# Expert coefficients by SBUF-to-SBUF transfers, the y chain in PSUM, and a new order of the loop

## What is computed

```
h = layernorm(x) * (1 + ca) + sa
q, k, v = h @ Wq + bq, h @ Wk + bk, h @ Wv + bv        # 16 heads of 8 channels
o = softmax(causal(q k^T / sqrt(8))) v
y = o @ Wo + bo
x = x + ga * (layernorm(y) * gamma + beta)
h = layernorm(x) * (1 + cb) + sb
p = softmax(h @ router)                                # 8 experts, the two largest kept: coef[t, e]
x = x + gb * (sum over e of coef[t, e] * (silu(h @ gate_e) * (h @ up_e)) @ down_e + shared expert)
```

## Time and profile before

| | us |
|---|---|
| three runs | 608.85, 610.38, 613.12 |
| median | 610.38 |
| the profiled execution's own time | 609.45 |
| its span, first to last instruction | 607.4 |
| TensorE busy | 521.5 |
| VectorE busy | 409.6 |
| ScalarE busy | 286.8 |
| GpSimd busy | 242.9 |

### The profile page before, as it was taken

The page is one execution under the profiler, slowest core; times in us unless marked ns, Lnnn a source line. Parts: engine busy times, 40 slices in busy tenths (PEclk is TensorE's granted clock), DMA queues, the critical chain, the costliest instruction groups (busy, mean ns, idle before and its releaser), DMA issues.

```text
span 607.4 us, 10186 instructions
## 1 busy us (share of the span) xinstructions
PE 521.5 (86%) x3627; PEld 277.3 (46%) x3635; DVE 409.6 (67%) x904; ACT 286.8 (47%) x582; POOL 242.9 (40%) x298
## 2 busy tenths in 40 slices
PE   1657798899998998889989998899989998999566
PEld 1523344454544464444544454455545464446234
DVE  6467875686677748787578757776778656873154
ACT  1103264645365555656354545565465636355311
POOL 6034115624274345623462427524562414242410
PEclk9956697989998999999998999999999999699769
DMA  5172313411233013411332113401341131001000
GB/s 139 55 183 76 108 41 76 144 41 40 64 92 123 12 47 81 146 32 41 93 121 63 41 50 84 144 2 43 89 145 41 41 74 42 2 2 37 0 1 17
DMA packets 46930, 40.65 MB, mean 67 GB/s; under 512 B 8088, under 2 KB 42656, under 8 KB 46880
## 3 DMA queue, kind: packets, MB, share of 16 engines
...
...
## 4 chain that ended last, share of the span: by engine, by line
PE 64%; DVE 19%; ACT 6%; issue 4%; POOL 3%; DMA 2%; SPq 1%; DVEq 0%; POOLq 0%
PE pv_bank L1023 10%; PE s_bank L1009 10%; PE s_bank L994 10%; DVE row_max L815 7%; PE gate_bank L1074 6%; PE gate_bank L1105 6%; PE up_bank L1083 5%; PE misc L952 4%; PE s_bank L996 4%; ACT probs L639 3%; PE misc L974 3%; DVE y_sb L851 2%; DVE stats_x L760 2%; ACT square L665 2%; PE misc L1045 1%
## 5 line engine op out<-in xcount | busy, mean ns | idle before, releaser
L815 DVE TENSOR_REDUCE row_max<-s_bank 128x1 f32<-128x512 f32 (+3 forms) x352 | 212.6, 636 | 47.0 <-PE s_bank L996 45.3
L639 ACT ACTIVATE probs<-s_bank 128x512 f32<-128x512 f32 x320 | 177.6, 595 | 54.4 <-PE s_bank L1009 51.6
L994 PE MATMUL s_bank<-k_stack,q_stack 72*128 72x256 bf16 (+3 forms) x512 | 139.1, 320 | 25.1 <-DVE row_max L815 13.9
L547 POOL TENSOR_SCALAR_AFFINE_SELECT probs<-probs 128x512 f32<-128x512 f32 (+1 forms) x96 | 77.6, 811 | 154.3 <-ACT probs L639 154.1
L1009 PE MATMUL s_bank<-q_stack,k_stack 75*128 75x128 bf16 (+3 forms) x512 | 115.0, 310 | 14.5 <-ACT probs L639 12.1
L996 PE MATMUL s_bank<-causal,ident_bf 128*128 128x128 bf16 x512 | 103.8, 229 | 0.0
L994 PEld LDWEIGHTS s_bank<-k_stack,q_stack 72*128 72x128 bf16 x512 | 51.9, 101 | 99.7 <-DVE row_max L815 66.3
L1023 PE MATMUL pv_bank<-probs,v_aug 128*32 128x512 f32 (+3 forms) x1024 | 95.3, 471 | 1.0
L1009 PEld LDWEIGHTS s_bank<-q_stack,k_stack 75*128 75x128 bf16 x512 | 40.0, 100 | 55.3 <-ACT probs L639 40.6
L648 ACT ACTIVATE u_sb<-pv_bank 128x512 f32<-128x512 f32 x32 | 19.1, 596 | 92.1 <-PE pv_bank L1023 92.1
L996 PEld LDWEIGHTS s_bank<-causal,ident_bf 128*128 128x128 bf16 x512 | 52.6, 103 | 15.7 <-issue 9.2
...
## 6 DMA issues: line engine op xcount, KB each, us to landing
...
```

Source lines behind the costliest of these rows:

```text
L547: nc.gpsimd.affine_select(out=view, in_=view, compare_op=ALU.is_ge, fill=0.0, base=0, pattern=pat, channel_multiplier=-1).then_inc(probs_r ...
L639: nc.scalar.activation(dst, src, ACT.Exp, scale=SCALE).then_inc(exp_done, 1)
L815: nc.vector.reduce_max(row_max[s % 2][:, 0, h:h + nh, qt], s1_bank[u % 2][:, 0:nh * w].rearrange("p (h k) -> p h k", h=nh), AX_X).then_inc ...
L994: nc.tensor.matmul(dst[:, w * i:w * (i + 1)], q_stack[0:KROWS, h, P * qt:P * (qt + 1)], k_stack[0:KROWS, h, 0:w], start=True, stop=False)
```

## The change

1. Coefficients. GpSimd's split is gone. PE transposes coef itself in float32 into rows 0 to 7 of misc, ACT copies these to coef_T (8 rows of 512). A new task cb on SyncE issues four transfers, one for each expert block: each reads two rows of coef_T, each row 64 times, and writes 128 rows of coef_b, 256 KB. The products with pick, ACT's copies to coef_sb and pick itself are gone. GpSimd (in the last batch DVE) multiplies hidden by coef_b when the block's own transfer has landed.
2. The y chain. PE first writes the bias into up_bank with one product of 65 rows of bfloat16 parts, then adds o @ Wo to it. ACT squares from the bank and also scales from the bank by the inverse deviation; DVE multiplies by gamma in one instruction (yg). u0 waits until y has left the bank.
3. The router product has 8 columns in place of 128.
4. The order: 30 steps in a slot in place of 15, s1, s2 and pv placed slot by slot, other tables EXTRA, LAST and LATER.

```diff
-    3: {0: [("c0", "prev")], 2: [("c1", "prev"), ("uev", "")],
-        3: [("g3", "prev"), ("c2", "prev"), ("u3", "prev")], 5: [("c3", "prev"), ("g4", "prev")],
-        6: [("u4", "prev")], 9: [("o", "")], 11: [("msplit", "cur"), ("down0", "prev")],
-        12: [("down1", "prev"), ("max", "cur")],
-        13: [("down2", "prev"), ("down3", "prev"), ("down4", "prev")], 14: [("fin", "prev")]},
...
+    3: {0: [("ct", "prev")], 3: [("u2", "prev")], 6: [("g3", "prev")], 7: [("cb", "prev")], 9: [("c0", "prev")],
+        13: [("c1", "prev")], 14: [("u3", "prev")], 16: [("g4", "prev")], 22: [("c2", "prev"), ("u4", "prev")],
+        23: [("uev", "")], 24: [("c3", "prev")], 26: [("down0", "prev")], 28: [("down1", "prev")],
+        29: [("msplit", "cur"), ("max", "cur"), ("down2", "prev"), ("down3", "prev"), ("down4", "prev"), ("fin", "prev"), ("o", "")]},
...
-STEPS = 15
-S1_STEPS = [0, 0, 2, 2, 3, 5, 5, 7, 8, 9, 10]
...
+STEPS = 30
+S1_STEPS = [[0, 1, 8, 9, 10, 12, 13, 16, 17, 18, 21],
...
-MISC_TASKS = ("o", "ot", "y", "x2t", "lg", "ct", "c", "xt", "q", "k", "v", "max")
+MISC_TASKS = ("o", "ot", "x2t", "lg", "ct", "xt", "q", "k", "v", "max")
...
+        bo_rest, bo_parts = sb("bo_rest", [P, PARTS, C]), sb("bo_parts", [P, T], BF16)
+        ones_bf = sb("ones_bf", [P, P], BF16)
...
-        pick = sb("pick", [P, FB, 2, DE], BF16)
...
-        coef_T = sb("coef_T", [P, T], BF16)
+        coef_T = sb("coef_T", [E, T])
         tanh_sb, silu_sb = sb("tanh_sb", [P, T]), sb("silu_sb", [P, T])
         hidden = sb("hidden", [P, MB, T])
-        coef_sb = sb("coef_sb", [P, T])
+        coef_b = sb("coef_b", [P, FB, T])
...
+                if name == "cb":
+
+                    need(sp, weighted, (it - 1) * FB)
+                    sp.wait_ge(misc_read, misc_at(it, (s_of(it, "ct"), "ct", 0)) + 1)
+                    for m in range(FB):
+                        sp.dma_start(coef_b[:, m, :],
+                                     coef_T[2 * m:2 * m + 2, :].unsqueeze(1).to_broadcast([2, DE, T])).then_inc(coef_spread[m], 16)
...
-                    pool.wait_ge(misc_read, misc_at(it, (s, "c", a)) + 1)
+                    pool.wait_ge(coef_spread[a], it * 16)
                     pool.wait_ge(up_read, it * MB + (a + 1 - MB))
-                    nc.gpsimd.tensor_tensor(hidden[:, a, :], hidden[:, a, :], coef_sb[:, :], ALU.mult).then_inc(weighted, 1)
+                    nc.gpsimd.tensor_tensor(hidden[:, a, :], hidden[:, a, :], coef_b[:, a, :], ALU.mult).then_inc(weighted, 1)
...
-                if name == "rank":
-
-                    c = coef[:, :, :]
-                    cp = [coef_parts[:, :, E * k:E * k + E] for k in range(PARTS)]
-                    need_all(pool, (const_done, 1), (coef_ready, it))
-                    nc.gpsimd.tensor_scalar(cp[0], c, 1.0, None, ALU.mult).then_inc(coef_step, 1)
-                    pool.wait_ge(coef_step, it * 3 - 2)
-                    nc.gpsimd.tensor_tensor(coef_rest[:, :, :], c, cp[0], ALU.subtract).then_inc(coef_step, 1)
-                    need_all(pool, (const_done, 1), (coef_step, it * 3 - 1))
-                    nc.gpsimd.tensor_scalar(cp[1], coef_rest[:, :, :], 1.0, None, ALU.mult).then_inc(coef_step, 1)
-                    pool.wait_ge(coef_step, it * 3)
-                    nc.gpsimd.tensor_tensor(cp[2], coef_rest[:, :, :], cp[1], ALU.subtract).then_inc(coef_split, 1)
...
-                    act.wait_ge(misc_read, misc_at(it, (s_of(it, "y"), "y", 0)) + 1)
+                    act.wait_ge(y_written, it)
                     for t in range(TT):
-                        final = nc.scalar.activation(square[:, t, :], y_sb[:, t, :], ACT.Square, accum_out=y_sq[:, t:t + 1])
+                        final = nc.scalar.activation(square[:, t, :], up_bank[:, P * t:P * (t + 1)], ACT.Square,
+                                                     accum_out=y_sq[:, t:t + 1])
                     final.then_inc(y_squares, 1)
+                if name == "yn":
+                    need(act, x2_ready, it - 1)
+                    act.wait_ge(y_rstd, it)
+                    for t in range(TT):
+                        final = nc.scalar.activation(y_sb[:, t, :], up_bank[:, P * t:P * (t + 1)], ACT.Copy,
+                                                     scale=rstd["y"][:, t:t + 1])
+                    final.then_inc(y_scaled, 1)
...
-                    nc.scalar.activation(coef_T[:, :], misc_bf[:, 0:T], ACT.Copy).then_inc(misc_read, 1)
-                if name == "c" and not last(it):
-
-                    act.wait_ge(misc_written, misc_at(it, (s, "c", a)) + 1)
-                    need(act, weighted, it * FB + (a - FB))
-                    nc.scalar.activation(coef_sb[:, :], misc[:, :], ACT.Copy).then_inc(misc_read, 1)
+                    for m in range(FB):
+                        need(act, coef_spread[m], it * 16 - 16)
+                    nc.scalar.activation(coef_T[:, :], misc[0:E, :], ACT.Copy).then_inc(misc_read, 1)
...
-                    nc.vector.tensor_tensor(bo_row[:, :], gate_bank[:, 0:C], bo_row[:, :], ALU.add).then_inc(centred, 1)
...
+                    dve.wait_ge(centred, 6 + PARTS)
+                    dve.wait_ge(const_step, CONST_STEPS)
+                    for r in range(PARTS):
+                        row = slice(PART_ROW * r, PART_ROW * r + 1)
+                        nc.vector.tensor_copy(bo_parts[row, :].rearrange("p (t c) -> p t c", t=TT),
+                                              upper(bo_rest[row, r, :]).unsqueeze(1).to_broadcast([1, TT, C])).then_inc(centred, 1)
...
-                if name == "y":
-                    k = misc_at(it, (s, "y", 0)) + 1
-                    dve.wait_ge(misc_written, k)
-                    if it == 1:
-                        dve.wait_ge(centred, 7)
-                    nc.vector.tensor_tensor(y_sb[:, :, :], misc_tok, over_tiles(bo_row[:, :]), ALU.add).then_inc(misc_read, 1)
-                if name == "yn":
-                    dve.wait_ge(y_rstd, it)
-                    for t in range(TT):
-                        final = nc.vector.scalar_tensor_tensor(y_sb[:, t, :], y_sb[:, t, :], rstd["y"][:, t:t + 1],
-                                                               gamma_a[:, it - 1, :], ALU.mult, ALU.mult)
-                    final.then_inc(y_scaled, 1)
+                if name == "yg":
+                    dve.wait_ge(y_scaled, it)
+                    nc.vector.tensor_tensor(y_sb[:, :, :], y_sb[:, :, :], over_tiles(gamma_a[:, it - 1, :]),
+                                            ALU.mult).then_inc(y_gamma, 1)
                 if name == "x2":
-                    dve.wait_ge(y_scaled, it)
+                    dve.wait_ge(y_gamma, it)
...
-                    dve.wait_ge(misc_written, misc_at(it, (s, "c", a)) + 1)
+                    dve.wait_ge(coef_spread[a], it * 16)
                     dve.wait_ge(up_read, it * MB + (a + 1 - MB))
-                    nc.vector.tensor_tensor(hidden[:, a, :], hidden[:, a, :], misc[:, :], ALU.mult).then_inc(misc_read, 1)
+                    nc.vector.tensor_tensor(hidden[:, a, :], hidden[:, a, :], coef_b[:, a, :], ALU.mult).then_inc(weighted, 1)
...
-                    take_misc(it, (s, "y", 0))
+                        pe.wait_ge(centred, BIAS_STEPS)
+                    need(pe, up_read, it * MB - MB)
+                    nc.tensor.matmul(up_bank[:, :], ones_bf[0:BO_ROWS, :], bo_parts[0:BO_ROWS, :], start=True, stop=False)
+                    pe.wait_ge(misc_read, misc_at(it, (s_of(it, "ot"), "ot", 0)) + 1)
                     for t in range(TT):
-                        final = nc.tensor.matmul(misc_tok[:, t, :], oT[:, P * t:P * (t + 1)], wo[:, :],
-                                                start=True, stop=True)
-                    final.then_inc(misc_written, 1)
+                        final = nc.tensor.matmul(up_bank[:, P * t:P * (t + 1)], oT[:, P * t:P * (t + 1)], wo[:, :],
+                                                start=False, stop=(t == TT - 1))
+                    final.then_inc(y_written, 1)
...
-                        final = nc.tensor.matmul(misc_tok[:, t, :], h2T[:, P * t:P * (t + 1)], w_router[:, :],
+                        final = nc.tensor.matmul(misc_tok[:, t, 0:E], h2T[:, P * t:P * (t + 1)], w_router[:, :],
...
-                    pe.wait_ge(coef_split, it)
+                    pe.wait_ge(coef_ready, it)
                     take_misc(it, (s, "ct", 0))
-                    transposes(misc_bf, lambda t: coef_parts[:, t, :], ident_bf).then_inc(misc_written, 1)
+                    transposes(misc[0:E, :], lambda t: coef[:, t, :], ident).then_inc(misc_written, 1)
...
+                    if a == 0:
+                        pe.wait_ge(y_scaled, it)
...
-                if name == "c":
-                    take_misc(it, (s, "c", a))
-                    nc.tensor.matmul(misc[:, :], pick[:, a, :, :].rearrange("p a b -> p (a b)"), coef_T[:, :],
-                                     start=True, stop=True).then_inc(misc_written, 1)
```

92 lines of the change are left out of this document (45 added, 47 removed), and 22 rows, old and new, of tables (LATER, S1_STEPS, S2_STEPS).

## The result

The change makes the kernel slower: median 849.2 us (846.6 to 852.5, four runs) against 611.0 for the kernel before in the same session, a ratio of 1.390 (95% interval 1.383 to 1.397). The forecast was 822, its range 660 to 860.

The account below looks back on a forecast made before the run. It took the kernel as bound by TensorE with VectorE handing it banks. The profiled 609.45 us, plus 186 for seven batches 26.6 us later each, plus 27 at the end, gave 822 us, range 660 to 860.

Parts of the forecast that it names:

- The pace of a transfer: Coefficient transfers: two rows put two of 16 engines to work at the slow pace, 9.4 us each, 37.6 for four.
- full pace: Rival, coefficient transfers: the engines keep full pace, 5.15 us each, four end 17.0 us earlier; 676 us, chance 0.14.
- spread over all engines: Rival, coefficient transfers: all engines at full pace, 0.66 us each, hidden, batch 3 us shorter; 587 us, chance 0.11.
- pace by the row: Rival, coefficient transfers: each source row sets the pace, 19.5 us each, 40 us more per batch; 1142 us, chance 0.05.
- The place: Fourth quarter of a batch: transfers follow third maxima and stack loads, down4 ends at 387.1 where before 360.46.
- The loop: Each batch 26.6 us later, gain and clock cancelling; seven times, 186 us.
- a term of 3: TensorE idle between down products falls to half clock: about 3 us a batch lost.
- The gain: Selection products gone, VectorE relieved by 2.4 us, new order: 3 us a batch saved, between nothing and 6.
- The end: Last batch: coefficients, four transfers of 37.6 us, one multiplication, down4, fin; span ends at 634.7, 27 us later.

Follow-up runs that it names:

- The pairs: Changed kernel with three copies of the coefficients, the four transfers reading rows 0 and 3, 8 and 10, 14 and 16, 19 and 21: 775.3 us.
- the two runs with eight rows: Changed kernel, each transfer reading eight source rows: neighbouring ones, from four copies of the coefficients, 659.5 us; every fourth of 32, from 16 copies, 588.4 us.
- 32 rows: Changed kernel with coefficients transposed in 16 copies, each transfer reading 32 rows four times each: 583.6 us, ratio 0.958 to the kernel before.
- the run with zero matrices: Changed kernel with 14 products of a 128 x 128 zero matrix before each of down2 to down4 in batches 0 to 6: 837.0 us.
- the old order: Kernel before with only the coefficient part, transfers from 32 source rows, c0 to c3 in steps 3 and 5 of the fourth slot: 612.4 us, ratio 1.000.

## Why the prediction was right

**The pace of a transfer: right, from the right row.** Two engines, 9.4 us each, was the term that held the forecast; it measured 10.1, the four 40.5 in place of 37.6. I had taken the slow pace from a transfer of 32 rows on the ground that the engines there drew on few neighbouring rows. The pairs and the two runs with eight rows show that this is the cause: rows of one group of four. The rival "full pace", 676 us, is what two rows 31 apart gave, 696.6: its mechanism is real, for other rows. So is "spread over all engines", 587 us: 32 rows gave 583.6, though at 1.4 us a transfer and not 0.66. The rival "pace by the row" is refuted by two far rows at 24 GB/s each.

**The place: right.** Issue, first packet and the end of the wait stood where the steps put them. From the issue of the third maxima to the end of the stack loads I had 5.1 us, it took 5.4; then 40.5 for 37.6; then GpSimd 1.3 and down4. The end of down4 came 49.2 us behind that issue where the sum had 45.1.

**The loop: the size was off, 31.2 us a batch for 26.6.** Of the 4.6 us, 2.9 are the transfers and 1.1 the last down product, 2.08 us at half clock where I had used 0.98 in that step and put the rest of the clock into a term of 3. The first three quarters did not get shorter (46.2 us for 46.8), where I had let a gain of 3 and a clock of 3 cancel; by the run with zero matrices the clock is 2.1 us a batch, its down4 included. The last 0.6 are small pieces. The sum also took the first fin for one of seven equal batches. It came 20.0 us later and not 26.6, since the 10.7 us that the new order gains ahead of it (next paragraph) hide a third of its delay. These 6.6 us of luck are part of why the total misses by 28 of 241 us: the six loop batches miss by 27.6 and the end by 6.4.

**The gain: near in sum, wrong in place.** With hidden transfers I had 587 us, and the 32-row kernel has 583.6. That the two lie so near is luck: I had 3 us a batch, and it is 2.3, all of it between the second and the third maxima (18.2 us for 20.5 on average); 10.7 us come before the first fin, which I had not looked at, and 2.1 at the end. Of those 10.7, 7.5 lie between the first and the second maxima of the first iteration, 21.1 us before and 13.6 with the new order, where no FFN and no y chain runs, so they belong to the order. Nor did the 3 us come from where I had them. Without the products the old order was no faster. And VectorE was not relieved: it is busy for 419 us with 32 rows, 409.6 before. Its scalings are gone, 17.6 us for 2.2 a batch, but the first step of splitting the maxima (L824 before, 419 ns at the mean) takes 923 ns in the new order, 16 us more in 32 instructions, and the copies of coef add 8.7 (10.2 us for 1.5). The split reads two arrays in SBUF. Here it is with the GpSimd instructions around it, in the kernel with 32 rows:

```profile
354.03 2.87 DVE L841 TENSOR_TENSOR row_max<-row_max 128x16 f32<-128x16 f32 x1
```
```profile
353.68 1.55 POOL L539 TENSOR_TENSOR wd_b<-wd,gate_b 128x640 f32<-128x640 f32 x1
355.18 1.70 POOL L561 TENSOR_SCALAR_AFFINE_SELECT probs<-probs 128x1024 f32<-128x1024 f32 x2
```

It ends at 356.90, GpSimd's last at 356.88; undisturbed the same instruction takes 0.17. In the kernel before one of 1.83 us ends at 305.81 beside a GpSimd series that ends at 305.79. So the instruction did not go ahead between the first GpSimd instruction and the two behind it. This is read from such records, not tested. (The Trainium skill, "SBUF — State Buffer", "Who interferes with whom", says that a VectorE instruction with two inputs in SBUF contends with a GpSimd instruction that reads SBUF; the records agree.) Why the new order loses 4 us a batch when the products are in it is shown only in part: TensorE, ScalarE and GpSimd wait for one another at c0 to c3, and from the third to the fourth maxima it takes 2.4 us longer than with 32 rows. Of the rest 1.0 lies between the second and the third maxima and 0.8 between the first and the second, much of it in single batches; it was not followed.

**The end: 33.6 us for 27.** The four transfers there end one by one under VectorE's multiplications, at 811, 822, 832 and 842, and each of the four down products that wait for them takes 2.07 us:

```profile
799.33 17.82 SPq L460 DMA_DIRECT2D coef_b<-coef_T  x4
811.19 0.69 DVE L920 TENSOR_TENSOR hidden<-hidden,coef_b 128x512 f32<-128x512 f32 x1 [4.38 <-DMA coef_b<-coef_T]
...
841.74 0.69 DVE L920 TENSOR_TENSOR hidden<-hidden,coef_b 128x512 f32<-128x512 f32 x1 [9.34 <-DMA coef_b<-coef_T]
```

From the previous fin (764.3) to the copy of coef_T are 35.0 us, where I had 33.1 (before, 36.1): 1.9 of the 6.4 us by which the end is longer than in the sum. The transfers are 3.1 more, 40.7 by the last multiplication, down4 at half clock 1.1, the first packet 0.2.

**The waits behind the wait.** The maxima of the fourth group did queue behind the coefficients, and SyncE with them (10.76 us for one issue), but in the whole execution TensorE's weight loads waited for max_rows 8.1 us, in 11 waits of at most 2.0, and its products 2.2 us; with 32 rows it was 6.5 and 1.6. That step cost next to nothing.

What carries the explanation is the kernel with four kinds of pairs, where only the rows read differ, and the two with eight rows (659.5 and 588.4), which differ in the rows read and the copies made. The rows written are the same in all of them. How the sharing is made, no run tells.
